# A transformer layer on one core: the second pair's maxima beside the first pair's exponentials, a token-major output projection, and new orders of the engines' steps

## The reference

```python
scores = Q @ K.T / sqrt(8) ; scores = where(j > i, -inf, scores) - (i - j)
x = layernorm(x + softmax(scores) @ V @ Wo.T + bo)
h = silu(tlin(x, w1)) * tlin(x, w2)          # 128 -> 512
h = gelu(tlin(h, h1)) ; h = gelu(tlin(h, h2))  # 512 -> 512, exact gelu
x = layernorm(x + tlin(h, w3))                 # 512 -> 128
```

## Time and profile before

| | |
|---|---|
| median of 3 runs | 860.47 us (860.15 to 861.4) |
| the profiled execution | 860.68 us |
| its span, first to last instruction | 858.0 us |
| granted TensorE clock, mean | 0.98 |
| busy: TensorE, VectorE, ScalarE, GpSimd | 92%, 78%, 61%, 54% |

### The profile page before, as it was taken

The page is one execution under the profiler, slowest core; times in us unless marked ns, Lnnn a source line. Parts: engine busy times, 40 slices in busy tenths (PEclk is TensorE's granted clock), DMA queues, the critical chain, the costliest instruction groups (busy, mean ns, idle before and its releaser), DMA issues. The chain is left out here.

```text
span 858.0 us, 18865 instructions
## 1 busy us (share of the span) xinstructions
...
## 2 busy tenths in 40 slices
...
GB/s 149 129 92 2 92 1 54 53 3 105 3 104 2 93 14 40 67 3 104 2 105 2 87 19 11 95 3 105 1 102 4 60 48 3 92 2 16 1 13 14
DMA packets 23185, 40.63 MB, mean 47 GB/s; under 512 B 2864, under 2 KB 4528, under 8 KB 23088
## 3 DMA queue, kind: packets, MB, share of 16 engines
...
...
## 5 line engine op out<-in xcount | busy, mean ns | idle before, releaser
L724 DVE CUSTOM_DVE_ANT_0 ps<-ps,causal 128x256 f32<-128x256 f32 (+1 forms) x1024 | 329.6, 392 | 51.3 <-PE ps L435 49.2
L892 POOL TENSOR_TENSOR hlo<-hf,hhi 128x512 fp32r<-128x512 f32 x192 | 246.6, 1285 | 208.8 <-ACT hhi L654 202.2
L598 ACT ACTIVATE pt<-ps 128x768 f32<-128x768 f32 x256 | 197.9, 808 | 61.6 <-PE ps L458 61.3
L867 POOL TENSOR_SCALAR_AFFINE_SELECT pt<-pt 128x512 f32<-128x512 f32 x256 | 164.4, 657 | 121.7 <-ACT pt L598 119.9
L646 ACT ACTIVATE hf<-ps,vec_sb 128x512 f32<-128x512 f32 x128 | 88.2, 689 | 133.4 <-PE ps L397 132.1
L391 PE MATMUL ps<-hhi,h_hi 128*128 128x512 f32 x512 | 157.1, 428 | 1.0 <-ACT hhi L654 1.0
L724 DVE DVE_READ_ACCUMULATOR2_ANT m<- 128x1 f32 x1024 | 143.5, 140 | 0.0
L397 PE MATMUL ps<-hlo,h_hi 128*128 128x512 f32 x512 | 139.1, 393 | 0.3 <-POOL hlo L892 0.3
L432 PE MATMUL ps<-ks,qs 32*128 32x256 f32 x512 | 92.5, 401 | 25.1 <-DVE m L724 20.8
L475 PE MATMUL ps<-pt,vst 128*32 128x256 f32 (+1 forms) x2048 | 107.1, 332 | 6.0 <-POOL pt L867 5.3
L397 PEld LDWEIGHTS ps<-hlo,h_hi 128*128 128x128 f32 x512 | 96.6, 189 | 23.5 <-POOL hlo L892 1.2
(11 more groups left out here) (102 smaller groups left out, 1002.2 us busy)
## 6 DMA issues: line engine op xcount, KB each, us to landing
...
```

The costliest lines, as they stand in the source:

```text
L598: nc.scalar.activation(pt[u][:, c:c + 2, :], ps[:, first:last + 1, 0:3 * P], ACT.Exp).then_inc(t_free.sem, 1)
L724: part = nc.vector.tensor_tensor_reduce(ps[:, bank, cols], ps[:, bank, cols], mask, 1.0, LOWEST, ALU.add, ALU.max, m32[:, it, c + e, u:u + 1])
L867: nc.gpsimd.affine_select(out=diag, in_=diag, compare_op=ALU.is_ge, fill=0.0, base=0, pattern=[[0, 2], [0, 2], [1, P]], channel_multiplier ...
L892: nc.gpsimd.tensor_tensor(h_lo[layer % 2][:, m, :], hf[:, n % 4, :], h_hi[layer % 2][:, m, :].bitcast(F32), ALU.subtract).then_inc(hlo_rea ...
```

## The change

- **Fill, slots, drain.** Each engine has three lists: `..._FILL` for the first two pairs, with pairs as numbers, `..._ORDER` for slots 2 to 15, `..._DRAIN` for the end. `steps` and `one_before` go.
- **Maxima of pair 1.** In the fill they are steps of one head, `s1` and `smax1` (b, n, e), in the two banks `FB` of the feed-forward net; they stand among pair 0's `st`, `exp` and `pv`. So `s` of pair 2 follows pair 1's `st` as before.
- **Start.** Three arrays gate the first projection instead of five; pair 0's k and v are projected in the banks `FB`; its stacks are written in halves, the first sequence's first.
- **wo token-major.** `wo` has tokens in partitions, so `zt 1` goes. x comes a second time, token-major (`tload`, `x_tok`); GpSimd adds the bias to it (`xbo`); `res1` adds the two; `lnstat 1` reads SBUF; `lnnorm 1` is GpSimd's. xT has two buffers instead of three.
- **Orders.** In `PE_ORDER` steps `s` and `st` stand in twos at 13 places (9 before, one of them an `s` with an `st`); `pv(1,2)` moves to the next slot, `gmul 3`, `ghi 3`, `glo 2`, `glo 3` and `hhi(1,1)` too; `qq` comes before `w3h`. SyncE sends `mTd(1,0)` and the store ahead of `kstack`. `table` steps stand behind the first exp and gelu of a slot.

```diff
+PE_FILL = [
+    ("qq", 0), ("qk", 0), ("qv", 0), ("qq", 1), ("s", 0, 0, 0), ("s", 0, 1, 0), ("s", 0, 2, 0), ("s", 0, 3, 0),
+    ("s", 0, 4, 0), ("s", 0, 5, 0), ("qk", 1), ("s", 0, 6, 0), ("s", 0, 7, 0), ("qv", 1), ("s", 1, 0, 0),
+    ("s", 1, 1, 0), ("s", 1, 2, 0), ("s", 1, 3, 0), ("mT", 0, 0), ("s", 1, 4, 0), ("s", 1, 5, 0),
+    ("s", 1, 6, 0), ("s1", 0, 0, 0, 1), ("s", 1, 7, 0), ("s1", 0, 0, 1, 1), ("st", 0, 0, 0), ("st", 0, 1, 0),
+    ("mT", 1, 0), ("s1", 0, 1, 0, 1), ("s1", 0, 1, 1, 1), ("st", 0, 2, 0), ("st", 0, 3, 0), ("s1", 0, 2, 0, 1),
+    ("s1", 0, 2, 1, 1), ("s1", 0, 3, 0, 1), ("st", 0, 4, 0), ("s1", 0, 3, 1, 1), ("st", 0, 5, 0),
+    ("s1", 0, 4, 0, 1), ("s1", 0, 4, 1, 1), ("st", 0, 6, 0), ("s1", 0, 5, 0, 1), ("st", 0, 7, 0),
...
+DVE_FILL = [
+    ("smax1", 0, 1, 0, 1), ("mTc", 1, 0), ("smax1", 0, 1, 1, 1), ("smax1", 0, 2, 0, 1), ("smax1", 0, 2, 1, 1),
+    ("smax1", 0, 3, 0, 1), ("smax1", 0, 3, 1, 1), ("smax1", 0, 4, 0, 1), ("smax1", 0, 4, 1, 1),
+    ("smax1", 0, 5, 0, 1), ("smax1", 0, 5, 1, 1), ("smax1", 0, 6, 0, 1), ("smax1", 0, 6, 1, 1),
...
+SP_FILL = [
+    ("xload", 1), ("wload", 0), ("kstack", 0, 0), ("qstack", 0, 0), ("qstack", 1, 0), ("kstack", 1, 0),
+    ("qstack", 1), ("tload", 0), ("kstack", 1), ("wload", 1), ("xload", 2), ("mTd", 0, 0), ("mTd", 1, 0),
...
 PE_ORDER = [
+    ("atT", 0, -1), ("s", 0, 0, 0), ("pv", 1, 2, -1), ("s", 0, 1, 0), ("pv", 1, 3, -1), ("s", 0, 2, 0),
+    ("h", 1, 0, -2), ("s", 0, 3, 0), ("s", 0, 4, 0), ("atr", 1, -1), ("h", 1, 1, -2), ("s", 0, 5, 0),
+    ("atT", 1, -1), ("h", 1, 2, -2), ("s", 0, 6, 0), ("s", 0, 7, 0), ("h", 1, 3, -2), ("wo", -1),
+    ("s", 1, 0, 0), ("s", 1, 1, 0), ("h", 2, 0, -2), ("h", 2, 1, -2), ("mT", 0, 0), ("s", 1, 2, 0),
+    ("s", 1, 3, 0), ("h", 2, 2, -2), ("s", 1, 4, 0), ("s", 1, 5, 0), ("x1t", -1), ("h", 2, 3, -2),
+    ("s", 1, 6, 0), ("s", 1, 7, 0), ("qq", 1), ("w3h", -2), ("st", 0, 0, 0), ("w3l", -2), ("st", 0, 1, 0),
+    ("st", 0, 2, 0), ("g", 0, -1), ("u", 0, -1), ("qk", 1), ("st", 0, 3, 0), ("pv", 0, 0, 0), ("g", 1, -1),
+    ("mT", 1, 0), ("st", 0, 4, 0), ("st", 0, 5, 0), ("zt", 2, -2), ("u", 1, -1), ("g", 2, -1), ("st", 0, 6, 0),
+    ("st", 0, 7, 0), ("pv", 0, 1, 0), ("pv", 0, 2, 0), ("u", 2, -1), ("st", 1, 0, 0), ("st", 1, 1, 0),
+    ("g", 3, -1), ("qv", 1), ("st", 1, 2, 0), ("st", 1, 3, 0), ("pv", 0, 3, 0), ("u", 3, -1), ("st", 1, 4, 0),
+    ("st", 1, 5, 0), ("atr", 0, 0), ("pv", 1, 0, 0), ("st", 1, 6, 0), ("st", 1, 7, 0), ("pv", 1, 1, 0),
 ]
...
 DVE_ORDER = [
+    ("gmul", 3, -2), ("ghi", 3, -2), ("smax", 0, 0, 0), ("smax", 0, 1, 0), ("smax", 0, 2, 0), ("smax", 0, 3, 0),
+    ("anorm", 1, -1), ("smax", 0, 4, 0), ("smax", 0, 5, 0), ("smax", 0, 6, 0), ("smax", 0, 7, 0), ("max", 0, 0),
+    ("res1", -1), ("smax", 1, 0, 0), ("smax", 1, 1, 0), ("lnstat", 1, -1), ("mTc", 0, 0), ("smax", 1, 2, 0),
+    ("smax", 1, 3, 0), ("smax", 1, 4, 0), ("smax", 1, 5, 0), ("x1lo", -1), ("smax", 1, 6, 0), ("smax", 1, 7, 0),
+    ("qlo", 0, 1), ("max", 1, 0), ("res2", -2), ("gate", 0, -1), ("qlo", 1, 1), ("gmul", 0, -1), ("mTc", 1, 0),
+    ("gate", 1, -1), ("ghi", 0, -1), ("lnstat", 2, -2), ("gmul", 1, -1), ("gate", 2, -1), ("lnnorm", 2, -2),
+    ("gmul", 2, -1), ("ghi", 1, -1), ("vadd", 1), ("araw", 0, 0), ("ghi", 2, -1), ("gate", 3, -1),
+    ("anorm", 0, 0),
 ]
 POOL_ORDER = [
+    ("glo", 2, -2), ("glo", 3, -2), ("hlo", 1, 0, -2), ("xbo", -1), ("hlo", 1, 1, -2), ("hlo", 1, 2, -2),
+    ("hlo", 1, 3, -2), ("rstd", 1, -1), ("lnnorm", 1, -1), ("hlo", 2, 0, -2), ("hlo", 2, 1, -2),
+    ("hlo", 2, 2, -2), ("hlo", 2, 3, -2), ("sel", 0, 0, 0), ("sel", 0, 1, 0), ("sel", 0, 2, 0),
+    ("sel", 0, 3, 0), ("sel", 0, 4, 0), ("sel", 0, 5, 0), ("rstd", 2, -2), ("sel", 0, 6, 0), ("glo", 0, -1),
...
 SP_ORDER = [
+    ("mTd", 0, 0), ("qstack", 1), ("xload", 2), ("mTd", 1, 0), ("store", -2), ("kstack", 1), ("tload", 0),
+]
+PE_DRAIN = [
+    ("pv", 1, 2, -1), ("atT", 0, -1), ("pv", 1, 3, -1), ("h", 1, 0, -2), ("atr", 1, -1), ("h", 1, 1, -2),
+    ("h", 1, 2, -2), ("atT", 1, -1), ("h", 1, 3, -2), ("wo", -1), ("h", 2, 0, -2), ("h", 2, 1, -2),
+    ("h", 2, 2, -2), ("x1t", -1), ("h", 2, 3, -2), ("g", 0, -1), ("u", 0, -1), ("w3h", -2), ("g", 1, -1),
+    ("u", 1, -1), ("w3l", -2), ("g", 2, -1), ("u", 2, -1), ("g", 3, -1), ("u", 3, -1), ("h", 1, 0, -1),
+    ("h", 1, 1, -1), ("h", 1, 2, -1), ("h", 1, 3, -1), ("zt", 2, -2), ("h", 2, 0, -1), ("h", 2, 1, -1),
...
+        def proj_bank(q, kind):
+            return {"qk": FB[0], "qv": FB[1]}.get(kind, ONE) if q == 0 else ONE
...
+        def wait_max_banks(eng, i, q):
+
+            if i >= 2:
+                s_free.wait(eng, max_pair(q), i - 1)
             else:
-                t_free.wait(eng, pair, n - 2 * HP - 1)
+                t_free.wait(eng, q - 1, 2 * HP - 1 + i)
+
+        def wait_first_max_bank(eng, i):
+
+            if i < 2:
+                qklo_ready.wait(eng, 0, 2)
+                v_ready.wait(eng, 0, 2)
             else:
+                eng.wait_ge(s1_free, i - 1)
...
+                    elif kind == "tload":
+                        zT_ready[0].wait(sp, q - 1)
+                        carry(sp, "sp")
+                        sp.dma_start(x_tok[:], xtok[q]).then_inc(xtok_loaded.sem, 16)
...
+                            part_cols, part_done = slice(s[1] * T, s[1] * T + T), half_stacked[s[1]]
...
+                        elif kind == "s1":
+                            _, b, n, e = s
+                            u, c, bank = n // 2, 2 * (n % 2) + e, FB[e]
...
+                            pe.matmul(ps[:, bank, 0:T], qr[:, P:T], kr, start=True, stop=False,
+                                      skip_group_check=True)
+                            pe.matmul(ps[:, bank, T:T + P], qr[:, 0:P], kr[:, 0:P], start=False,
+                                      stop=True, skip_group_check=True).then_inc(s1_full, 1)
...
-                            pe.matmul(ps[:, ONE, :], wo_sb[:], attT[:], start=True, stop=True
-                                      ).then_inc(l_full.sem, 1)
+                            for j in range(TT):
+                                last = pe.matmul(ps[:, ONE, j * P:(j + 1) * P], attT[:, j * P:(j + 1) * P],
+                                                 wo_sb[:], start=True, stop=True)
+                            last.then_inc(l_full.sem, 1)
...
+                    elif kind == "smax1":
+                        _, b, n, e = s
+                        u, c, bank = n // 2, 2 * (n % 2) + e, FB[e]
+                        dve.wait_ge(s1_full, 2 * (HP * b + n) + e + 1)
...
+                        part.then_inc(s1_free, 1)
...
-                        nc.vector.scalar_tensor_tensor(
-                            out=zT[0][:], in0=ps[:, ONE, :], scalar=vec_sb[:, 2:3],
-                            in1=xT[q % 3][:], op0=ALU.add, op1=ALU.add).then_inc(zT_ready[0].sem, 1)
+                        xb_ready.wait(dve, q)
+                        ln_part[0].wait(dve, q - 1)
+                        nc.vector.tensor_tensor(zT[0][:], ps[:, ONE, :], x_tok[:].rearrange("p j d -> p (j d)"),
+                                                ALU.add).then_inc(zT_ready[0].sem, 1)
...
+                        src = ps[:, ONE, :] if n else zT[0][:]
...
+                    elif kind == "xbo":
...
+                        nc.gpsimd.tensor_tensor(x_tok[:], x_tok[:], bo_sb[:].unsqueeze(1).broadcast_to([P, TT, D]),
+                                                ALU.add).then_inc(xb_ready.sem, 1)
+                    elif s == ("lnnorm", 1):
+                        l_full.wait(pool, q - 1)
+                        carry(pool, "pool")
+                        ln_rstd[0].wait(pool, q)
+                        for j in range(TT):
+                            nc.gpsimd.tensor_scalar(
+                                x1[:, j, :], zT[0][:, j * P:(j + 1) * P], mv[0][:, j, 0:1],
+                                rstd[0][:, j:j + 1], ALU.subtract, ALU.mult).then_inc(ln_part[0].sem, 1)
...
-PROJ_LOADS = 5
+PROJ_LOADS = 3
```

More of the change, by code:

```diff
@@ L84 @@
+    ("exp", 1, 3, 0), ("exp", 1, 4, 0), ("exp", 1, 5, 0), ("exp", 1, 6, 0), ("exp", 1, 7, 0), ("araw", 1, 0),
+    ("attT", 0, 0), ("gelu", 1, 0, -1), ("table", "gelu", 0), ("hhi", 1, 0, -1), ("gelu", 1, 1, -1),
 ]
 DVE_ORDER = [
-    ("smax", 0, 0, 0), ("smax", 0, 1, 0), ("smax", 0, 2, 0), ("smax", 0, 3, 0), ("anorm", 1, -1),
-    ("smax", 0, 4, 0), ("smax", 0, 5, 0), ("smax", 0, 6, 0), ("smax", 0, 7, 0), ("res1", -1), ("max", 0, 0),
-    ("smax", 1, 0, 0), ("lnstat", 1, -1), ("smax", 1, 1, 0), ("smax", 1, 2, 0), ("lnnorm", 1, -1),
@@ L89 @@
-    ("smax", 1, 3, 0), ("mTc", 0, 0), ("smax", 1, 4, 0), ("smax", 1, 5, 0), ("smax", 1, 6, 0), ("x1lo", -1),
-    ("smax", 1, 7, 0), ("res2", -2), ("w_mx", 2), ("qlo", 0, 1), ("max", 1, 0), ("gate", 0, -1),
-    ("gmul", 0, -1), ("ghi", 0, -1), ("qlo", 1, 1), ("gate", 1, -1), ("mTc", 1, 0), ("gmul", 1, -1),
-    ("lnstat", 2, -2), ("ghi", 1, -1), ("gate", 2, -1), ("lnnorm", 2, -2), ("gmul", 2, -1), ("ghi", 2, -1),
```

(5 more changed lines are left out.)

521 lines of the change are left out of this document (320 added, 201 removed), and 31 rows, old and new, of tables (DVE_FILL, PE_DRAIN, PE_FILL, PE_ORDER).

## The result

| kernel | median | runs | ratio to the kernel before, 95% interval |
|---|---|---|---|
| before | 860.31 us | 4 | |
| changed | 878.06 us (875.88 to 878.92) | 4 | 1.0200 [1.0178, 1.0222] |

A forecast was written before the change was run, and what follows sets the result against it. TensorE was taken to pace the slots, with VectorE runner-up and bounding parts of the fill. From 858.0 us, slots -28.0, fill -11.1 and drain -3.5 gave 815.4 of span, plus 2.7 around it: 818 us, range 803 to 838.

The forecast's parts named there:

- the sentence on GpSimd: Slots: four 128x128 norm instructions on GpSimd at 0.33 us each, 1.3 for the four, ended before TensorE reaches x1t.
- slack of 0.5: Slots: GpSimd's norm ends some 0.5 us before TensorE reaches the x1 transposes.
- R3: Slots: shared SBUF access lets new GpSimd work stretch VectorE, +0.6 us a slot, 854 us; chance 0.03.
- R4: Slots: GpSimd's four norm instructions cost 1.285 us each, TensorE stands 3.3 us, 864 us; chance 0.04.
- the price of the twos: Slots: pairing score steps saves 0.37 us per two of s, 0.42 per two of st, 1.95 in all.
- the drain: Drain: w3h and w3l between gates, norm moved, zt 1 gone, pv(1,2) added; together -3.5 us, bounds 0 and -6.
- Waits of the twos: Slots: TensorE waits for VectorE to free both bank pairs before a two; net +0.6 us a slot.
- The term for s(1,5): Slots: 0.5 us of wait at s(1,5), where lnstat 1 and mTc stand in front of its bank's maxima.
- R1: Slots: VectorE takes over and the twos return their saving except half a microsecond, 832 us; chance 0.24.
- The fill: Before the first slot: overlapping pair 1's maxima with pair 0's exponentials and an earlier start; -11.1 us, bounds -2 to -16.
- the overlap: Fill: pair 1's maxima beside pair 0's exponentials take 35.4 us instead of 46.0, -10.6 before the +1.5 correction.
- the one for the one-head banks and the half-speed matmuls: Fill: one head per bank makes TensorE answer each release in 0.63 us, often missed; +1.5 us, bounds 0 to +8.

The follow-up runs named there:

- e1: Changed kernel with the first normalization moved from GpSimd back to VectorE, behind the maxima of group (1,3); 880.37 us.
- e4: Changed kernel with one swap in ScalarE's order, hhi(1,1) ahead of gelu(1,2), so GpSimd's three subtractions are spread; 838.09 us.
- e7: e5 with GpSimd's first subtraction of the second layer held until VectorE's four normalization steps are done; 815.44 us.
- e5: Changed kernel with the swap of e4 and the normalization on VectorE as in e1; 840.66 us.
- e3: Changed kernel with ten useless matmuls a slot in TensorE's idle time, four ahead of s(1,4), six ahead of the x1 transposes; 849.58 us.
- e8: Changed kernel with the swap of e4 and the ten filler matmuls of e3; 825.78 us.
- e6: e4 with the first normalization's statistics directly behind the residual sum, ahead of the maxima of groups (1,0) and (1,1), on VectorE; 808.84 us.
- e9: e6 with eight of its twos taken apart, seven st steps and one s step each put one step later; 857.99 us.

## Why the prediction was wrong

**The step that failed** is the sentence on GpSimd: "I take 0.33, near the lower end ... the norm then ends some 0.5 us before TensorE reaches `x1t`". One of the four takes 0.796 us, so the four take 3.13 in place of 1.3. By the prediction's own slack of 0.5 that alone gives a wait of 1.3 us; 1.6 were measured. The value lay inside the bounds 0.24 to 1.285, but the two ends were treated as if the lower one were the likelier, on the ground of fewer columns; nothing but a row of that form could tell. Taking this price away is not enough: in e1 the norm left GpSimd and nothing was gained, since on VectorE it came late and took 2.17 us. What the price is worth once `max` is on time, e4 and e7 show: with an undisturbed norm of 1.11 us a slot falls from 47.70 to 46.13 us, the clock's share included. No run has an undisturbed norm in the changed kernel's own order.

**What the step left out** are two costs that have no term in the sum.

*Contention.* R3 named the mechanism, gave it 0.03 and argued it away with medians taken in the kernel before. Medians in the old order say nothing of the new one: the new orders put three subtractions back to back beside `max`, which then takes 2.06 us instead of 0.47 in each slot. R3 was wrong, too, in hanging the cost on the 2.6 us that GpSimd gains: the subtractions were there before, it is their new place that counts, and this place is set by ScalarE's order (`hhi(1,1)` behind `gelu(1,2)`), which the prediction read only for what it hides. That the subtractions are the cause is shown by e4, where `max` takes 0.47 us again, and for the norm by e5 and e7, 2.06 against 1.11 us. The Trainium skill (GPSIMD Engine Reference, section Key points) says that GpSimd shares its SBUF interfaces with VectorE, with contention for VectorE's instructions in a 2-port mode or with two SBUF inputs. The trace agrees for the second instruction of `max`, which has two inputs in SBUF and takes 1.28 us beside a subtraction and 0.17 without; whether the norm and the first instruction of `max`, with one tensor in SBUF, ran in a 2-port mode, no run shows.

*The clock.* The prediction priced waits at their own length. Behind these waits TensorE's clock fell from 2.4 to 1.2 GHz in all 14 slots, so that `h(2,3)` took 3.0 to 3.8 us in place of 2.1, and e3 shows that this cost 2.16 us a slot, more than the longest wait. R4 had the right place and the wrong price: it asked for 1.2 us apiece; with lateness and clock added, 0.8 was enough.

**The sum, mended.** e3, e8 and e6 take the 4.92 us between the changed kernel's slot and e6's apart, in this order: clock 2.16, bunched subtractions 48.36 - 46.82 = 1.54, norm too late 46.82 - 45.60 = 1.22. Another order would share them out otherwise, since they feed one another. In all it is 14 x 4.92 = 69 us, the whole distance from 878 to 809.

**Right.** The work that the change takes off TensorE: a slot of e6, which has this work and nearly no waits, takes 45.60 us, against 46.6 forecast and 46.1 by content alone (48.62 - 2.54). TensorE's busy time in the 14 slots is 631.41 us in e6 and 667.79 before: (667.79 - 631.41) / 14 = 2.60 us less a slot, where the prediction's parts add up to 2.54. e9 confirms the price of the twos, the largest item. `wo` cost nothing (a record of 1.05 us where 1.13 stood), and the drain came out at -3.3 against -3.5. Table loads stood behind waits as forecast, and GpSimd's `xbo` was hidden.

**Waits of the twos.** +0.6 a slot was forecast; s(0,7) and s(1,5) were named. In the changed kernel three maxima waits of 0.23, 0.33 and 0.82 us stand at s(1,3) to s(1,5), none at s(0,7), and e6 has none in that slot. The term for s(1,5) was right in itself: in e4, with `max` on time, one wait is left, 0.46 us at s(1,5), against 0.5 forecast there for `lnstat 1` and `mTc` ahead of its maxima, and it goes when e6 moves `lnstat 1`. The 0.4 at s(0,7) did not come. R1 (VectorE takes over) did not come about: it is late by contention, not by work.

**The fill.** -6.8 against -11.1. The start gained 2.8 (first score matmul at 17.32 instead of 20.13 us), more than the 2.0 assumed, so the overlap brought 4.0 instead of 9.1. The term that was too small is the one for the one-head banks and the half-speed matmuls, for which 1.5 was set, with bounds up to 8: it came to 10.6 - 4.0 = 6.6. The prediction read a low clock only from 64 us on; but the score matmuls take 0.59 us from 20 us on the earlier trace rows, against 0.38 in the slots, so the first part of the fill was slow as well (the last section says why the clock column hides it). TensorE is busy for 53.5 us between 17.3 and 88 us at a clock of 0.50 to 0.68; that it, rather than the alternation of single banks, is the cause was not shown. Also open is the share of contention in the fill, which was not tried by itself: its four `max` steps take 3.30, 2.02, 0.76 and 0.47 us, against 2.44, 0.47, 0.47 and 0.46 before, 2.7 us more in all.
